# The tail of a fused matrix attention kernel: eight loads of a prepared weight from ScalarE's queue, issued one after the other instead of between the first pair's splits

## The reference

```python
x = x + einsum('bct,bcd->bdt', x, w0[idx])
q, k, v = proj(x, Wq), proj(x, Wk), proj(x, Wv)      # 1024 x 1024 each
scores = (q * min(cond, 4)) @ k.T / 8                # causal mask, 16 heads
x = x + (softmax(scores) @ v) @ Wo.T
```

## Time and profile before

| | us |
|---|---|
| median of three runs | 1571.56 |
| lowest and highest | 1571.53, 1573.22 |
| the profiled execution | 1573.44 |
| its span, first to last instruction | 1572.1 |
| TensorE busy in it | 1560.5 |
| mean granted clock of TensorE | 0.999 |

### The profile page before, as it was taken

The page is one execution under the profiler, slowest core; times in us unless marked ns, Lnnn a source line. Parts: engine busy times, 40 slices in busy tenths (PEclk is TensorE's granted clock), DMA queues, the critical chain, the costliest instruction groups (busy, mean ns, idle before and its releaser), DMA issues.

```text
span 1572.1 us, 23424 instructions
## 1 busy us (share of the span) xinstructions
PE 1560.5 (99%) x7563; PEld 1311.5 (83%) x7563; DVE 980.2 (62%) x1748; ACT 818.6 (52%) x2221; POOL 856.7 (54%) x752
## 2 busy tenths in 40 slices
PE   9999999999999999999999999999999998999999
PEld 7888888888888888888888888888888876888887
DVE  5844454443367777777766777777777654555553
ACT  6645545543366666666666666666666621222220
POOL 1545645643255566557655566675577544555552
PEclk9999999999999999999999999999999999999999
DMA  9958888865866666767677466666665696444442
GB/s 325 338 209 276 306 285 296 300 218 217 304 184 193 208 204 201 209 193 193 184 241 235 154 176 209 192 189 194 192 180 154 232 353 240 167 161 164 164 162 86
DMA packets 192299, 341.46 MB, mean 217 GB/s; under 512 B 23986, under 2 KB 116402, under 8 KB 185010
## 3 DMA queue, kind: packets, MB, share of 16 engines
q1 hardware_dynamic: 191026, 331.59, 65.6%
q10 hardware_dynamic: 1152, 8.39, 1.3%
HBM read 184.70 MB, written 134.22 MB: 203 GB/s over the span
## 4 chain that ended last, share of the span: by engine, by line
PE 95%; DMA 3%; SPq 1%; POOL 0%; DVE 0%; issue 0%; ACT 0%; DVEq 0%; POOLq 0%; ACTq 0%
PE p_PJ L710 22%; PE p_PJ L711 22%; PE p_PJ L712 22%; PE p_SC L710 6%; PE p_SC L712 6%; PE p_SC L711 6%; PE p_PV L815 4%; PE p_PV L710 1%; PE p_PV L712 1%; PE p_PV L711 1%; DMA out<-t_LATE 1%; PE p_LP L710 1%; PE p_LP L712 1%; PE p_LP L711 1%; DMA t_LATE<-x_scratch 1%; PE p_PV L841 1%
## 5 line engine op out<-in xcount | busy, mean ns | idle before, releaser
L711 PE MATMUL p_PJ<-t_XL,t_WH 128*128 128x512 f32 x1008 | 394.1, 391 | 0.0
L710 PE MATMUL p_PJ<-t_XH,t_WH 128*128 128x512 f32 x1008 | 394.1, 391 | 0.0
L712 PE MATMUL p_PJ<-t_XH,t_WL 128*128 128x512 f32 x1008 | 392.1, 389 | 0.0
L1035 ACT ACTIVATE t_PP<-t_PP,t_st 128x128 f32<-128x128 f32 x512 | 199.5, 391 | 174.5 <-DVE t_st L1211 173.0
L1333 POOL TENSOR_TENSOR t_PP<-t_PP,t_st 128x512 f32<-128x512 f32 x128 | 133.4, 1042 | 204.9 <-DVE t_st L1215 204.9
L712 PEld LDWEIGHTS p_PJ<-t_XH,t_WL 128*128 128x128 f32 x1008 | 189.3, 188 | 40.4
L710 PEld LDWEIGHTS p_PJ<-t_XH,t_WH 128*128 128x128 f32 x1008 | 190.0, 189 | 33.8
L711 PEld LDWEIGHTS p_PJ<-t_XL,t_WH 128*128 128x128 f32 x1008 | 190.0, 188 | 32.3
L1229 DVE TENSOR_REDUCE t_AT<-p_PV 64x256 f32<-64x512 f32 x252 | 171.2, 680 | 20.8 <-ACT t_AC L1053 12.0
L1339 POOL TENSOR_TENSOR t_AT<-t_AT,t_AC 128x256 f32<-128x256 f32 x126 | 117.2, 930 | 122.7 <-DVE t_AT L1229 122.7
L1336 POOL TENSOR_TENSOR t_PS<-t_PT,t_PS 128x512 fp32r<-128x512 f32 x122 | 157.8, 1293 | 0.0
(11 more groups left out here) (254 smaller groups left out, 3547.9 us busy)
## 6 DMA issues: line engine op xcount, KB each, us to landing
t_XH<-xth_scratch SPq DMA_DIRECT2D x56, 512.0 KB, 6.6
t_XL<-xtl_scratch SPq DMA_DIRECT2D x56, 512.0 KB, 7.0
t_PT<-t_TB SPq DMA_DIRECT2D x580, 32.0 KB, 2.4
v_scratch<-t_VR SPq DMA_DIRECT2D x64, 256.0 KB, 4.4
xth_scratch<-t_XH SPq DMA_DIRECT2D x16, 1024.0 KB, 4.0
xtl_scratch<-t_XL SPq DMA_DIRECT2D x16, 1024.0 KB, 6.3
t_VX<-v_scratch SPq DMA_DIRECT2D x32, 512.0 KB, 5.6
at_scratch<-t_AT SPq DMA_DIRECT2D x126, 128.0 KB, 3.4
```

The source lines that it names most:

```text
L710: pe.matmul(bank, lh, rh, start=first, stop=False, skip_group_check=goes_on)
L711: pe.matmul(bank, lh, rl, start=False, stop=False, skip_group_check=goes_on)
L712: return pe.matmul(bank, ll, rh, start=False, stop=last, skip_group_check=goes_on)
L1035: act.activation(PP[:, u, h, :], PP[:, u, h, :], ACT.Exp, bias=st[:, 0, u, h:h + 1], scale=1.0, accum_out=st[:, 1, u, h:h + 1]).then_inc(a ...
```

## The change

Four due times. Wo's pieces 6, 5, 4 and 7 are now fetched at T_END + 26.5, 29, 31.5 and 34 in place of 27, 40, 50 and 62:

```diff
         for k, high, low in ((3, -38.5, -54.5), (1, -22.5, -22.5), (0, -6.5, -6.5), (2, 9.5, 9.5),
-                             (6, 27, 27), (5, 40, 40), (4, 50, 50), (7, 62, 62)):
+                             (6, 26.5, 26.5), (5, 29, 29), (4, 31.5, 31.5), (7, 34, 34)):
             O_fetch.put(T_END + high, (k, 0))
             O_fetch.put(T_END + low, (k, 1))
```

## The result

| us | before | after |
|---|---|---|
| median | 1572.32 (5 runs) | 1579.58 (5 runs) |
| lowest, highest | 1571.53, 1573.22 | 1578.48, 1580.34 |
| the profiled execution | 1573.44 | 1579.52 |
| its span | 1572.1 | 1578.2 |

The change makes the kernel slower: the ratio is 1.0047, with a 95% interval of 1.0036 to 1.0058, 7.3 us by the medians. The two profiled executions are 6.1 us apart; before's, at 1573.44, took longer than any of its five other runs.

A forecast was written before the change was run, and what follows sets the result against it. TensorE bound the kernel, losing 7.1 us in a tail chain of DMAs. Restart at 1300.9 plus 24.5 us of matmuls plus 1.7 clock gave 1327.1 against 1321.4, +5.7 us: 1577.3 us, range 1569.5 to 1583.0.

The forecast's parts named there:

- pair 0's data there: Landing of t_PP and t_PT, the first pair's attention output, as seen by ScalarE: 1297.0 instead of 1281.3, 15.7 us later.
- addition of the fifth turn ends: VectorE's addition that empties the PJ bank the eighth output turn needs: ends at 1300.8 instead of 1285.1.
- stop of the eighth turn: TensorE reaches the eighth output turn at 1289.8 and stands still for its bank until 1300.9: 11.1 us.
- cost of the granted clock: TensorE's lower clock after the idle stretch, taken as the same 1.7 us as in the earlier trace.
- waits on p_SC: TensorE's three tail waits on the banks of the first pair's products, 2.0, 1.8 and 1.0 us: all covered.
- pair 1 begins later by: Start of TensorE's pair 1 moves from 1321.4 to 1327.1, +5.7 us, and shifts the end equally.
- The packet count: SyncE's q1 and ScalarE's q10 alternate one packet each; 1488 q1 packets through t_PT end at 1295.9.
- Shared by bytes: Rival: q1 gets half the bytes beside q10, pair 0's data is not late, 1564.5 us; chance 0.12 including any landing before 1288.
- Longer turns: Rival: engines take several packets per turn, t_PT lands near 1291.5, 1571.8 us; chance 0.15 including any landing between 1288 and 1294.
- The cover for ScalarE's issues: ScalarE's six moved-up load issues fit in slack of 1.9 and 2.3 us around its copies, adding nothing.
- VectorE's order: On VectorE the fifth turn's addition stands behind two low halves awaiting pair 0's data, 3.8 us from landing to its end.
- the point from which the change loses: Break-even landing of t_PT at 1291.3: earlier the change wins, later it loses, one for one.

The follow-up runs named there:

- the fetches behind the copies: Changed kernel with Wo pieces 5, 4 and 7 issued only behind the second copy of the last values: 1572.03 us, 0.9997 of the kernel before.
- The run with two pieces more: Kernel before with Wo pieces 5 and 4 also moved up and piece 7 left at 62, 6.3 MB issued early: 1575.89 us, ratio 1.0025.
- the one that landed at 1287.0: Kernel before with only Wo piece 5 also moved up, pieces 4 and 7 left at 50 and 62: 1573.96 us, ratio 1.0012.

## Why the prediction was right

Step by step, forecast and measured:

| | forecast | measured |
|---|---|---|
| pair 0's data there | 1297.0 | 1297.2 |
| addition of the fifth turn ends | 1300.8 | 1300.9 |
| stop of the eighth turn | 11.1 | 11.1 |
| cost of the granted clock | 1.7 | 2.2 |
| waits on p_SC | none | none |
| pair 1 begins later by | 5.7 | 6.2 |
| time | 1577.3 | 1579.58 |

**The packet count** was the step on which all hung, and it held: packet for packet. The equal counts stood in the earlier trace rows, a whole load of q1 beside q10 did not; 4-KB packets took q1 from 49 to 83 packets per us, which the byte rule excludes and the turn rule asks for. *Shared by bytes* is out: q1 moved 0.94 MB beside 6.12 MB. *Longer turns* is out: t_PT, 32 packets on each engine, landed at 1297.2 and not at 1291.5. The Trainium skill, page "DMA: Bandwidth & Descriptors", section "Queues, rings and completion order", has engines drain a whole packet of typically 9 to 17 descriptors from one queue before they switch. The going round is what these runs show; that a long transfer gets on faster than a short one, as this rival took from it, they do not show.

The landing is right within 0.2 us in part by luck. Of the 1488 packets that the prediction counts, q1 had moved 1418 by 1295 and 293 more by 1296, so the last of them went near 1295.2, not 1295.9; but ScalarE started 1.9 us after that, not 1.1. In the kernel before, with 1306 packets by 1280 and 347 in the next microsecond, the same distance is 0.8 us. The counts of one queue over all engines don't tell when the slowest engine is through: q10's own last three packets of 8 KB started one by one, 0.35 us apart, until 1295.4.

**The cover for ScalarE's issues** held: the copies were where they had been.

**VectorE's order** carried the lateness to the eighth turn, as said. What the prediction left out is that this coupling is not needed for the loss: without it the products waited instead, to the same end.

**The clock** was mis-sized. I took the 1.7 us of the earlier trace rows; the window 1301 to 1308.5 had 0.71 in the mean, so 0.29 x 2 x 7.5 = 4.4 us at the lower level, and half of it, 2.2 us, was lost. The run with spare matmuls puts it at 2.1 us (24.6 us from the eighth turn to pair 1, against 26.7).

**The number** is 2.3 us low. 0.5 us of it is the clock. 0.8 us is the median I started from: 1571.56 of three runs, where five gave 1572.32. The remaining 1.0 us is the distance between 6.1 us in the profiled pair and 7.3 by the medians, less rounding: before's profiled execution, from which the rows are taken, was 1.1 us slower than its median. Runs of one kernel spread over 1.7 to 1.9 us, and I have no cause for it.

**What the prediction had wrong without harm.** It let a load take turns from its issue on, where in these runs it began 3 to 4 us later with the other queue in full work. In the changed kernel each load had the earlier ones ahead of it and q10 never stood idle, so the sum was right; for the fetches behind the copies the same reasoning gave 1580, and the chip 1572. Why the first packets come so late these runs don't tell: whether the descriptors are made late or stand behind the other queue's was not tried.

It also set the point from which the change loses too late. By it a landing at 1291.3 costs nothing and an earlier one wins. The run with two pieces more landed there and was slower by 0.25% (some 4 us), and the one that landed at 1287.0 by 0.12%. Both kept part of the waits that the prediction struck out, 1.6 and 4.2 us on p_SC; in both, pieces fetched later still moved beside the last stores. In the changed kernel q10 was through by 1296, and those waits were gone. No run with a landing before 1291.3 was clearly faster than the kernel before.

## What to carry to other kernels

Before you move a bulk load ahead, look at who shares the DMA engines with it: beside a stream of large packets a queue of small ones got one packet for one here, so count its packets, not its bytes, and follow the last one to the engine that waits for it. A gap in the bulk queue just where the urgent loads run is worth more than an early start; here one 2-MB piece issued 2.3 us earlier closed it and cost 8 us. Where all engines are busy from end to end, what one transfer gains the next one in the chain can lose, as it did in several orders here, so follow the chain to its end before you count a gain.

## What was unexpected of the hardware

- A load issued while the other queue was in full work got its first packets some 3 to 4 us after its issue: 1275.4 to after 1279, 1281.5 to after 1285 and, with hardly a gap in its queue, 1273.1 to 1276.8 on q10; 1290.8 to after 1294 and 1302.8 to after 1306 on q1. With the other queue idle or at the end of its last load it was 1.0 to 1.3 us. The gap that this makes is no margin to build on: with one set of fetch times it was wide enough for t_PT in one kernel and too narrow in another (1281.4 and 1286.3).
- An issue on SyncE grew long when its queue was backed up. Two loads of Y took 1.10 us to issue in the kernel before; in after, with the same two loads:

```profile
1283.72 9.75 SPq L1586 DMA_DIRECT2D t_Y<-at_scratch  x2
```

  SyncE's next issue came only at 1293.51. Nothing urgent stood behind it here, since x1 of the eighth turn was waiting for a store in any case. ScalarE's issues, with up to eight loads of 8-KB rows in its queue, never took over 0.53 us in after; with 4-KB pieces its last ones took 1.2 to 1.8 us.
